# RWKV time mix and channel mix in four token blocks: the blocks enter one by one, the engines' lists are reordered, and a block's result is summed on VectorE before it is turned

## The reference, cut to what matters

```python
x_prev = concatenate([x[:, :1], x[:, :-1]], axis=1)
kvr = _layernorm(x, g1, b1) @ W_tm
k, v, r = split(kvr, 3)
k = k * tmk + x_prev * (1.0 - tmk)            # v and r likewise, r through a sigmoid
y, new_state = _wkv(time_decay, time_first, k, v)   # recurrence over the 256 tokens
x = x + r * y
xp = concatenate([x[:, -1:], x[:, :-1]], axis=1)
xn = _layernorm(x, g2, b2)
kk = (xn @ W_cm) * cmk4 + xp4 * (1.0 - cmk4)  # 512 wide
rr = sigmoid(xn * cmr + xp * (1.0 - cmr))
x = x + rr * (square(relu(kk)) @ W_cp)
```

## Time and profile before

| what | us |
|---|---|
| median of 3 runs | 847.23 (842.67 to 850.68) |
| the profiled execution: its time | 846.06 |
| its span, first to last instruction | 844.3 |
| last add_out of the first FFN ends | 130.25 |
| first running_max of the RWKV stage starts | 150.60 |
| first instruction of the next FFN starts | 285.92 |
| busy over the span: PE, DVE, ACT, POOL | 699.9, 562.8, 409.6, 317.0 |

### The profile page before, as it was taken

One profiled execution on the slowest core, in us unless ns is written; L12 is line 12 of the kernel. 1 busy time (PEld: TensorE's weight loads), 2 busy tenths in 40 slices (PEclk: granted clock), 3 DMA queues, 4 the chain that ended last, 5 costly groups with the idle time before them and its releaser, 6 DMA issues. The chain is left out here.

```text
span 844.3 us, 12326 instructions
## 1 busy us (share of the span) xinstructions
PE 699.9 (83%) x3996; PEld 514.5 (61%) x3996; DVE 562.8 (67%) x1283; ACT 409.6 (49%) x747; POOL 317.0 (38%) x398
## 2 busy tenths in 40 slices
PE   0979992626766699999999976699999997699997
PEld 0657762222242367777777856677777775477785
DVE  3668673454475578889887766655565655688785
ACT  2545663554312155555555544655555553355554
POOL 1436786000001156664654553232222210264455
PEclk9989995857787899999999996699999998799999
DMA  5335530000000033232212210000000000032222
GB/s 143 86 110 163 162 100 0 1 0 0 0 2 0 0 101 101 91 90 72 102 51 83 76 43 0 1 1 2 2 0 0 0 0 2 31 115 69 78 88 75
DMA packets 32757, 43.10 MB, mean 51 GB/s; under 512 B 5184, under 2 KB 15424, under 8 KB 32704
## 3 DMA queue, kind: packets, MB, share of 16 engines
q1 hardware_dynamic: 32704, 42.46, 16.4%
HBM read 41.13 MB, written 1.31 MB: 50 GB/s over the span
## 5 line engine op out<-in xcount | busy, mean ns | idle before, releaser
L503 POOL TENSOR_TENSOR p_prod<-p_p,p_gate_row 128x512 f32<-128x512 f32 x128 | 201.0, 1579 | 148.0 <-DVE p_p L389 97.1
L303 ACT ACTIVATE p_sil<-p_ps_a 128x512 f32<-128x512 f32 x176 | 105.2, 598 | 144.8 <-PE p_ps_a L100 141.0
L394 DVE TENSOR_TENSOR p_hlo<-p_prod,p_hhi 128x512 fp32r<-128x512 f32 x176 | 148.1, 843 | 1.7 <-ACT p_hhi L312 1.4
L389 DVE TENSOR_TENSOR p_p<-p_sil,p_ps_b 128x512 f32<-128x512 f32 x128 | 87.4, 683 | 66.7 <-ACT p_sil L303 53.7
L312 ACT CAST p_hhi<-p_prod 128x512 fp32r<-128x512 f32 x176 | 107.9, 613 | 21.7 <-POOL p_prod L503 21.6
L98 PE MATMUL p_ps_acc<-p_hhi,w_downhi 128*128 128x512 f32 x176 | 71.6, 407 | 4.1 <-DVE p_hlo L394 4.0
L98 PE MATMUL p_ps_a<-xt_hi,w_uphi 128*128 128x512 f32 x176 | 75.0, 426 | 0.0
L98 PE MATMUL p_ps_b<-xt_hi,w_uphi 128*128 128x512 f32 x176 | 71.6, 407 | 0.3 <-DVE p_prod L389 0.3
L100 PE MATMUL p_ps_b<-xt_hi,w_uplo 128*128 128x512 f32 x176 | 70.7, 402 | 0.0
L99 PE MATMUL p_ps_b<-xt_lo,w_uphi 128*128 128x512 f32 x176 | 70.6, 401 | 0.0
L99 PE MATMUL p_ps_a<-xt_lo,w_uphi 128*128 128x512 f32 x176 | 70.6, 401 | 0.0
(11 more groups left out here) (277 smaller groups left out, 1445.2 us busy)
## 6 DMA issues: line engine op xcount, KB each, us to landing
p_gate_row<-gate_rows SPq DMA_DIRECT2D x128, 256.0 KB, 3.2
w_rawbuf<-in_L_ffn_fc_w_dram SPq DMA_DIRECT2D x3, 512.0 KB, 6.1
w_rawbuf<-in_L_ffn_w_dram SPq DMA_DIRECT2D x3, 512.0 KB, 5.8
out_dram<-x SPq DMA_DIRECT2D x4, 256.0 KB, 3.7
w_rawbuf<-in_L_ffn_shared_w_dram SPq DMA_DIRECT2D x3, 256.0 KB, 4.8
mb_xraw<-in_L_attn_W_B_dram SPq DMA_DIRECT2D x1, 512.0 KB, 4.9
mb_xraw<-in_L_attn_W_C_dram SPq DMA_DIRECT2D x1, 512.0 KB, 5.0
gate_rows<-p_gates_t SPq DMA_DIRECT2D x16, 16.0 KB, 1.4
```

Source lines behind the costliest of these rows:

```text
L303: nc.scalar.activation(sil[:, u % 2], ps_a[:, u % 2], ACT.Silu).then_inc(c["sil"].sem, 1)
L389: nc.vector.tensor_tensor(dst, sil[:, u % 2], ps_b[:, u % 2], ALU.mult).then_inc(c["p1"].sem, 1)
L394: nc.vector.tensor_tensor(hlo[:, u % R], prod[:, u % R], hhi[:, u % R].bitcast(F32), ALU.subtract).then_inc(c["hlo"].sem, 1)
L503: G.tensor_tensor(prod[:, u % R], p1[:, u % 2], gate_row[:, e % ROWS], ALU.mult).then_inc(c["prod"].sem, 1)
```

## The change

- In the first FFN's last block DVE also prepares the parameter vectors (step 1), the mixing matrices (step 2) and the statistics of RWKV blocks 0 and 1 (steps 3 and 4); POOL scales them at steps 6 and 7; ACT makes the tokens of block 0 at step 8, ahead of take_out, and those of block 1 behind it. SPLIT_SLOTS move.
- The scales of a block take 3 dependent steps of POOL with one power operation of 8 columns (before: 7 dependent steps with two power operations for two blocks); scale2 takes 3 steps (before 4).
- take_in becomes take_y and take_z, factors gives its tanh to a new item thresh, shifted becomes shifted_k and shifted_r, and moments and moments2 join measure and measure2.
- turn_x2 writes to the key bank of its block, turn_z2 to its value bank, turn_out to grown[2]. grow waits only for the shift of two before it.
- gated is followed by summed (DVE): tg = 0.5 tg + x2; turn_out is then 4 transpositions of tg. half_ident is gone. shift gets a wait for the square of two before.
- All lists are in another order.

```diff
-    SPLIT_SLOTS = {(2, 6): 0, (2, 7): 1, (3, 5): 2, (3, 6): 3, (3, 7): 4, (3, 8): 5}
+    SPLIT_SLOTS = {(2, 5): 0, (2, 6): 1, (2, 7): 2, (3, 0): 3, (3, 3): 4, (3, 5): 5}
...
+                    if entry and (n, p) == (BLOCKS - 1, U - 2):
+                        next_tokens(0)
                 take_out(n)
+
+            def next_tokens(m):
+                act.wait_ge(c["r_rs"].sem, c["r_rs"].at(m + 1))
+                apply_norms(nc, x, entry, m).then_inc(c["r_tok"].sem, 1)
...
             for n in range(BLOCKS):
                 body(n)
+            if entry:
+                next_tokens(1)
...
+            def next_stage(p):
+                if p == 1:
+                    prepare_vectors(nc, dve, c, entry["vec"])
+                if p == 2:
+                    prepare_mixing(nc, dve, c, entry["vec"], consts, entry, entry["weights"])
+                if p in (3, 4):
+                    m = p - 3
+                    take_stats(nc, x, entry, m).then_inc(c["r_st"].sem, 1)
+                    dve.wait_ge(c["r_st"].sem, c["r_st"].at(m + 1))
+                    take_moments(nc, entry, m).then_inc(c["r_mom"].sem, 1)
...
+                    if entry and n == BLOCKS - 1 and p in (U - 4, U - 3):
+                        scale_norms(nc, pool, c, consts, entry, p - (U - 4))
...
+def scale_norms(nc, pool, c, consts, entry, m):
...
+    pool.wait_ge(c["r_mom"].sem, c["r_mom"].at(m + 1))
+    G.tensor_scalar(r[:, 0], var, LN_EPS, None, ALU.add)
+    G.tensor_scalar(r[:, 1], var, 1.0 + LN_EPS, LN_EPS * LN_EPS, ALU.mult, ALU.add)
+    G.tensor_scalar(r[:, 4], mean, -1.0, None, ALU.mult).then_inc(c["r_c1"].sem, 1)
+    pool.wait_ge(c["r_c1"].sem, c["r_c1"].at(2 * m + 1))
+    G.tensor_tensor(r[:, 2:4].rearrange("p a b -> p (a b)"), r[:, 0:2].rearrange("p a b -> p (a b)"),
+                    consts["minus_half"][:, 0:2 * BT], ALU.pow).then_inc(c["r_c1"].sem, 1)
+    pool.wait_ge(c["r_c1"].sem, c["r_c1"].at(2 * m + 2))
+    G.tensor_tensor(r[:, 5:7], r[:, 2:4], r[:, 4:5].broadcast_to([P, 2, BT]), ALU.mult).then_inc(c["r_rs"].sem, 1)
...
             def turn_out(m):
                 h = m % 2
-                pe.wait_ge(c["r_gate"].sem, c["r_gate"].at(m + 1))
-                pe.wait_ge(c["r_tr"].sem, c["r_tr"].at(4))
-                if m:
-                    pe.wait_ge(c["r_out"].sem, c["r_out"].at(m))
+                pe.wait_ge(c["r_sum"].sem, c["r_sum"].at(m + 1))
                 for j in range(BT):
-                    b, s = j // 2, j % 2
-                    part = mixed[4][:, bass.ts(j, P)]
-                    pe.matmul(part, x2[h][:, b, 1 + s * P:1 + (s + 1) * P], ident[:], start=True, stop=False)
-                    last = pe.matmul(part, tg[h][:, bass.ts(j, P)], half_ident[:], start=False, stop=True)
+                    last = pe.transpose(grown[2][:, bass.ts(j, P)], tg[h][:, bass.ts(j, P)], ident[:])
                 last.then_inc(c["r_ot"].sem, 1)
...
+            def summed(m):
+                h = m % 2
+                dve.wait_ge(c["r_gate"].sem, c["r_gate"].at(m + 1))
+                V.scalar_tensor_tensor(out=seqs(tg[h][:]), in0=seqs(tg[h][:]), scalar=0.5, in1=mid(x2[h]), op0=ALU.mult,
+                                       op1=ALU.add).then_inc(c["r_sum"].sem, 1)
```

More of the change, by code:

```diff
@@ L1105, in _ @@
-            parts(1, "r_g", "r_low")
-            total(0)
+            parts(1)
+            lead2(0)
+            parts2(0)
+            numerator(0)
+            numerators(0)
+            apart(0)
             total(1)
-            lead2(0)
+            blend(0)
+            output(0)
+            received(0)
+            residual(0)
             lead2(1)
-            parts(0, "r_g2", "r_low2")
-            parts(1, "r_g2", "r_low2")
-            numerator(0)
+            parts2(1)
+            measure2(0)
@@ L1132, in _ @@
+            square(0)
             running_max(2)
+            lead(2)
+            parts(2)
+            shift(1)
+            square(1)
+            total(2)
+            shift(2)
+            square(2)
+            gate_in(1)
+            lead2(2)
+            parts2(2)
+            shift(3)
+            square(3)
+            numerator(2)
             running_max(3)
-            lead(2)
+            numerators(2)
             lead(3)
-            gate_in(0)
-            parts(2, "r_g", "r_low")
@@ L1138, in _ @@
-            gate_in(1)
-            parts(3, "r_g", "r_low")
-            shift(0)
-            shift(1)
-            square(0)
-            total(2)
-            square(1)
-            shift(2)
-            total(3)
-            square(2)
-            shift(3)
-            lead2(2)
-            square(3)
+            apart(2)
+            parts(3)
+            gated(0)
+            summed(0)
+            blend(2)
+            total(3)
+            output(2)
+            shift(4)
+            received(2)
@@ L1151, in _ @@
+            residual(2)
+            wrap(2)
             lead2(3)
-            shift(4)
-            parts(2, "r_g2", "r_low2")
-            parts(3, "r_g2", "r_low2")
+            add_out(0)
             square(4)
             shift(5)
-            numerator(2)
-            gated(0)
-            numerator(3)
+            parts2(3)
             square(5)
             shift(6)
-            numerators(2)
+            measure2(2)
             square(6)
+            shift(7)
+            numerator(3)
@@ L1195, in _ @@
             square(11)
+            wrap(3)
+            gated(2)
+            summed(2)
+            gate_in(3)
+            add_out(2)
             shift(12)
+            shift(13)
             square(12)
-            shift(13)
             square(13)
-            gated(2)
             shift(14)
+            shift(15)
             square(14)
-            add_out(2)
-            shift(15)
             square(15)
             gated(3)
+            summed(3)
             add_out(3)
@@ L1213, in _, with scale @@
             half = consts["minus_half"]
[L1215 to L1235 removed]
+            def scale(m):
+                scale_norms(nc, pool, c, consts, entry, m)
             def scale2(m):
```

416 lines of the change are left out of this document (208 added, 208 removed).

## The result

The kernel after the change takes 801.1 us, the median of 4 runs (796.01 to 802.41), against 844.95 us (841.87 to 850.68, 4 runs) for the kernel before: a ratio of 0.946, with a 95% interval of 0.939 to 0.953. The profiled execution took 801.08 us, with a span of 799.4 and a mean granted clock of 0.928. The forecast was 804.

A forecast was written before the change was run, and what follows sets the result against it. The RWKV stage was taken to be bound by engines waiting for each other, none full. Body 38.2 plus entry 5.9 gave 44.1 off the profiled 846.06, so 802.0; with handoffs 804, range 793 to 823.

The forecast's parts named there:

- the three orders that I had named: ACT's list before the change: logs behind receive 1, factors behind tokens 2 and 3, second pair's key product behind take_in 2.
- the entry: From the FFN's last block to the first scan: first running_max at 144.7 instead of 150.60, worth 5.9 us, range 3 to 10.
- the body: From first running_max to last add_out: 135.0 us before, 96.8 after, a gain of 38.2.
- the 2.0 added for handoffs: Some 40 handoffs between engines of 0.05 us, taken as zero in the walk, raised the sum from 802.0 to 804.
- the bound of 129: Latest time for POOL to be free in the FFN's last block, if weighings stretch beside a split; 127.5 was expected.
- Transpositions instead of accumulated matmuls: turn_out with fewer PE instructions: 0.7 us gained once at the end, while DVE pays 2.0 of 2.7 us for summed.
- at nothing: DVE's added vectors and statistics in the FFN, about 4.3 us of work, cost nothing; 2 us if POOL were not late.
- PE sets the pace: Rival: PE at 1.2 GHz after running_max 2 needs 80 us instead of 59; 814 to 832 us, chance 0.22.
- my walk: Hand trace of the four engine lists through the stage in trace durations: running_max 2 at 37.8, end at 96.8.
- Only part of the order works: Rival: items too early hold ACT 5 to 7 us per pair; 818 to 824, sharing 0.22; four waits, 832 to 839, 0.05.
- The lists leave the blocks end to end: Rival: four RWKV blocks of 45 us each run one after another, 180 us against 153; 878 us, chance 0.02.
- The change does less than it says: Rival: statistics ahead of the barrier win nothing, the entry is worth 0; 810 us, inside the main case, no separate chance.

The follow-up runs named there:

- experiment 2: The changed kernel with the lists of PE, ACT and DVE put back to the order in pairs of blocks: 839.8 us, ratio 0.994.
- experiment 6: The changed kernel with decays 1 ahead of receive 1 and tokens 3 moved behind shifted_r 1 in ACT's list: 797.5 us, ratio 0.943.
- Experiment 8: The changed kernel with the last three splits off POOL, their low parts on DVE behind its last low part: 799.45 us, one execution.
- experiment 3: The changed kernel without summed, turn_out again accumulating x2 and half of tg by matmuls: 805.16 us, ratio 0.954.
- experiment 1: The changed kernel with the preparation for blocks 0 and 1 back in the stage and the splits in their old slots: 801.02 us, ratio 0.950.
- experiment 5: The changed kernel with 14 matmuls more, whose results nobody reads, to keep PE busy in the first half: 797.17 us, one execution.
- experiments 1 and 7: 7: the changed kernel with take_out ahead of tokens 0, tokens 1 behind the stage change, turn_in 1 behind mix_val 0: 805.08 us.

## Why the prediction was right, point by point

**The mechanism** is shown by experiment 2: the time was waits, the order of the lists made them, and with the old order 40.0 of the 46.6 us come back. That single misplaced items of ACT cost microseconds is shown by experiment 6. How the 40 us divide among the three orders that I had named (receive 1 ahead of logs, tokens ahead of factors, take_in 2 behind the shifted and tokens2 items) was not tried.

**The sizes.** The sum was 804, measured 801.1. That it came within 3 us is in part luck, since two terms were off in opposite directions: the entry won 2.0 us less than forecast and the body 4.5 more, the 2.0 added for handoffs were not there, and the unchanged stretch behind the stage took 1.7 longer (804 + 2.0 - 4.5 - 2.0 + 1.7 = 801.2).
- The entry was over-sized: 5.9 us forecast, 3.9 measured (first scan 146.71, forecast 144.7). POOL was free at 130.0, not 127.5. The splits took 5.3 us (5.2 forecast) and the weighings 13.1 (12.5), but I had let POOL run without a gap, and it waited 2.4 us (1.67 and 0.76). That came of a misread row: I took "[1.53 <-DVE p_p L389]" at 109.11 for DVE waiting for a late POOL, but it is POOL that waited there for DVE's product, and before the change it idled ahead of each of the last five weighings as well (0.17 to 0.48 us), while DVE waited for POOL once (1.28 us, at 110.96). So POOL was not late, and DVE's added work, costed at nothing because POOL was thought late, reached it through the products. Experiment 8 shows the same two gaps, and three more, with the splits gone. What DVE's additions cost apart from the splits was not run. The scales took 3.35 us instead of 2.65. So the stage opened at 140.5 instead of 137.3. PE gave 1.2 us back: its clock rose within mix_key 0, so turn_in to the scan took 6.2 us and not 7.4. That POOL's path from the last weighing sets the opening was right; the bound of 129 was a microsecond short.
- The body was under-sized: 38.2 us forecast, 42.7 measured (96.8 down to 92.3). running_max 2 came at +35.0 instead of +37.8: logs 0 was done at +9.3 (10.4 forecast), and take_z 2 at +32.4 (34.4). residual 3 ended at +70.1 instead of 75.0, 4.9 ahead; the tail behind it took 22.2 us, forecast 21.8. The 2 us that I had added for handoffs were not there. Of the waits that I saw in the second half, about 6.6 us, DVE shows 4.5.
- Two details came out as forecast, within 1 us: mix_rec 1 at the low clock until +15.1 (forecast 16.1), and nine table loads at 1.28 us.

**Single claims.** "Transpositions instead of accumulated matmuls" was wrong in its sign: I had it as a cost of 1.3 us, and experiment 3 measured a gain of 2.35, because I looked for its effect only in the last block. (It is also 16 instructions that become 4, not 16 pairs.) I missed the wait of residual 3 on the buffer that turn_out 1 reads, and I charged DVE's additions in full although DVE had idle time beside most of them. DVE busy near 76 us: 78.1. The vectors, matrices and statistics "at nothing" did not hold in the FFN, as said above; experiment 1, which takes them out together with all else that was moved, shows only that the whole move nearly cancels out.

**The rivals.** "PE sets the pace" asked for a low clock after running_max 2; it was 0.97, and 0.76 with the old lists (experiment 2), so PE's clock came with the filled gaps. In the first half it was 0.71, and experiment 5 prices that at 2.4 us, within my walk. "Only part of the order works" is true on a small scale: tokens 3 and receive 1 were written too early, as experiment 6 shows, and cost 3.4 to 4.5 us together, not 5 to 7 each. "The lists leave the blocks end to end" had no place: DVE idles 14 us in all. "The change does less than it says" was right in its mechanism and wrong in its time: the work moved into the FFN is worth 0.3 us (experiment 1), yet the first scan still came 2.8 us earlier without it (experiment 1), and the time was 801, not 810, because the body won more.

**Table loads.** Nine loads at 1.28 us: at 163.48 a load follows the exponential that ended at 163.47, and the logarithm starts at 164.78, 1.31 us in all. The 2.66 us of the Trainium skill (ScalarE: Activation LUTs, section What ACT_TABLE_LOAD costs) are a load of 1283 ns and a drain of 1380: the load agrees with the 1.28 us of the trace, the drain is not seen here. By its price the four extra loads would have cost 10.6 us, and the body is shorter than the sum with 5.1. That a load stands between a logarithm (187.75) and the exponentials (load at 189.62) says which tables this program loads; it does not speak against a set that holds both, as my prediction had it.

## What to carry to other kernels

Where engines work through lists in order and none is full, look for items that wait, and ask what stands behind them in the same list: here writing the items block by block, with work of another block behind each long wait, turned 41 us of idle time into 40 us of time. An earlier first result is worth only what the next block can follow (experiments 1 and 7). Read a bracket as the idle time of the engine in its own row, and ask for each engine whether it is full before you add work to it: DVE had 4.4 us free in 14.6 us of the FFN's last block, and the added work left it none. Count a wait from the side of the last user, and look for each buffer that a step frees, in every block and not only the last.

## What the runs showed of the hardware

- DVE and POOL held each other up, even in tiny operations. An operation on one column with two inputs, 0.15 us in the neighbouring row of its kind (experiment 1, at 134.50), took 2.04 us at 114.75 and ended with POOL's split (113.84 to 116.78). A low part that takes 0.68 alone took 2.32 beside the next split. The other way round, POOL's scale step at 130.07 took 0.77 instead of 0.23, and its power operation 2.49 instead of 1.67, each beside two-input DVE work. The Trainium skill (SBUF — State Buffer, section Who interferes with whom) says that a DVE operation with two SBUF inputs contends with a GpSimd operation that reads SBUF, and calls the ports that they share an exclusive lock. The rows agree: 129.88 plus 1.22 for DVE's split, then 1.67, gives 132.8 for the power operation that ended at 132.6. Of the 0.70 us that the scales took more than forecast (3.35 for 2.65), the step at 130.07 has 0.54.
- PE's clock after a gap: behind a gap of 4.48 us mix_rec 1 ran at the low level (2.07 and 1.91 us for the two groups), behind one of 1.61 us at the high level (1.13 and 1.02), with the same work ahead of it.
- The stretch behind the stage, with the same code, took 554 to 561 us in these executions, so a single time can be 6 us off. The position of the last add_out told the edits apart to about a microsecond: the kernel of experiment 6 had it at 234.88 and at 233.86, and the starts differ by up to 1.2 us. Lengths between two points of the stage agree better: the second half took 57.16 to 57.53 us in the nine executions that have the changed kernel's lists there.
